# Cross part by single groups: ten chains merged by one list of turns, one or two banks per group

## The reference

```
x = x + xattn(layernorm(x), ctx)

xattn(y, Z):
  y = layernorm(y + attention(y, y, y, causal), g1, beta1)
  y = layernorm(y + attention(y, Z, Z),         g2, beta2)
  h = relu(y @ w1 + b1)                      # 128 -> 512
  y = layernorm(y + h @ w2 + b2,                g3, beta3)
```

## Time and profile before

| | |
|---|---|
| time, median of 3 runs | 762.5 us (760.36 to 763.86) |
| the profiled execution's own time | 763.72 us |
| its span, first to last instruction | 761.9 us |
| mean granted TensorE clock | 0.853 |
| busy: PE / DVE / ACT / POOL | 625.3 / 461.8 / 256.4 / 97.1 us |
| cross part, until XA is complete | about 112 us |
| DVE goes on after the trip through HBM | 123.7 us |

### The profile page before, as it was taken

How to read it: one execution, slowest core, us unless ns; L and a number is a source line. 1 busy time by engine, 2 the same in 40 slices (tenths; PEclk the granted TensorE clock), 3 DMA queues, 4 the chain that set the end, 5 groups by cost and what they waited for, 6 DMA issues and landing times.

```text
span 761.9 us, 15678 instructions
## 1 busy us (share of the span) xinstructions
PE 625.3 (82%) x6640; PEld 427.1 (56%) x6640; DVE 461.8 (61%) x1124; ACT 256.4 (34%) x555; POOL 97.1 (13%) x140
## 2 busy tenths in 40 slices
PE   2777951786899999694997699978888799999995
PEld 1434641475688858464796678776444344444442
DVE  5846694978966354748828822475556855555552
ACT  1455510742421623642632034214323122222221
POOL 2535452300000001301100001010011000000000
PEclk9888985955599999897768658976899999999998
DMA  9994021000000000000000050000032163333321
GB/s 343 291 375 160 1 83 29 0 2 2 2 3 4 3 1 3 0 3 0 2 3 2 2 178 2 2 2 1 0 80 65 57 161 94 96 97 108 88 81 28
DMA packets 18981, 46.68 MB, mean 61 GB/s; under 512 B 3456, under 2 KB 8192, under 8 KB 18656
## 3 DMA queue, kind: packets, MB, share of 16 engines
q1 hardware_dynamic: 18368, 45.43, 19.3%
q10 hardware_dynamic: 544, 0.26, 0.1%
HBM read 43.32 MB, written 2.36 MB: 60 GB/s over the span
## 4 chain that ended last, share of the span: by engine, by line
PE 66%; DVE 22%; ACT 3%; DMA 3%; POOL 2%; issue 2%; SPq 1%; DVEq 0%; POOLq 0%
PE psum L753 7%; PE psum L748 7%; PE psum L758 7%; PE psum L685 5%; PE psum L594 5%; PE psum L560 3%; PE psum L711 3%; PE psum L714 3%; PE psum L674 3%; PE psum L621 3%; PE psum L667 2%; PE psum L720 2%; PE psum L571 2%; DVE yr L1287 2%; PE psum L464 2%; DVE pcT L1287 2%
## 5 line engine op out<-in xcount | busy, mean ns | idle before, releaser
L932 ACT ACTIVATE arena<-psum 128x512 f32<-128x512 f32 x68 | 40.6, 598 | 136.0 <-PE psum L748 122.9
L1363 DVE TENSOR_TENSOR arena<-psum,arena 128x512 f32<-128x512 f32 x64 | 44.2, 691 | 59.6 <-PE psum L753 57.8
L758 PE MATMUL psum<-arena,wed_sb 128*128 128x512 f32 x128 | 66.8, 604 | 0.0
L776 ACT ACTIVATE arena<-psum 128x512 f32<-128x512 f32 x56 | 33.3, 600 | 69.7 <-PE psum L560 41.0
L1368 DVE TENSOR_TENSOR arena<-arena 128x512 f32<-128x512 f32 x64 | 44.3, 692 | 14.0 <-PE psum L758 13.8
L560 PE MATMUL psum<-arena 32*64 32x128 f32 x1024 | 41.9, 327 | 6.6 <-ACT arena L776 2.8
L952 POOL TENSOR_TENSOR ve<-ss,eps_rms 128x4 f32<-128x4 f32 x16 | 3.7, 230 | 340.5 <-ACT yr L827 252.9
L560 PEld LDWEIGHTS psum<-arena 32*64 32x64 f32 x1024 | 36.8, 165 | 12.6 <-ACT arena L776 4.1
L753 PE MATMUL psum<-yT,weu_sb 128*128 128x512 f32 x68 | 36.3, 616 | 7.9 <-DVE arena L1363 7.9
L758 PEld LDWEIGHTS psum<-arena,wed_sb 128*128 128x128 f32 x128 | 24.6, 192 | 31.3 <-issue 22.7
L1314 DVE TENSOR_TENSOR arena<-psum,small 128x1024 f32<-128x1024 f32 x24 | 28.2, 1214 | 14.2 <-PE psum L667 14.2
(11 more groups left out here) (283 smaller groups left out, 1290.2 us busy)
## 6 DMA issues: line engine op xcount, KB each, us to landing
arena<-shares SPq DMA_DIRECT2D x64, 256.0 KB, 3.9
arena<-in_ctx_t SPq DMA_DIRECT2D x16, 514.0 KB, 8.9
arena<-in_ctx_z SPq DMA_DIRECT2D x16, 512.0 KB, 10.5
XA<-in_x SPq DMA_DIRECT2D x1, 1024.0 KB, 5.1
zlast<-in_ctx_last SPq DMA_DIRECT2D x4, 256.0 KB, 17.7
x_mid<-XA SPq DMA_DIRECT2D x4, 256.0 KB, 3.0
weg_sb<-in_we_gate SPq DMA_DIRECT2D x2, 512.0 KB, 6.5
weu_sb<-in_we_up SPq DMA_DIRECT2D x2, 512.0 KB, 7.5
```

The source lines that it names most:

```text
L758: pe.matmul(x3, wed_sb[:, (p - 1) % (NPAIR + 1), :], act_a[pr], start=(p == 0), stop=False, skip_group_check=True).then_inc(x_down[pr], 1)
L776: return act.activation(out_, in_, ACT.Copy, scale=scale)
L932: act.activation(act_g[pr], banks[4 * pr + 2 * (n % 2)], ACT.Silu).then_inc(x_silu[pr], 1)
L1363: dve.tensor_tensor(act_gu[pr], banks[4 * pr + 1], act_g[pr], ALU.mult).then_inc(x_gu[pr], 1)
```

## The change

The list's steps become steps of single groups. Each pair has five chains: `BEFORE` for each of its two groups (st0 to nm1 and ev1), the attention steps c, and `AFTER` for each group (cr to fin). ev1, ev2 and fin are split off: the ACT copy to zT after the transposes (ev1, ev2), and the last update of XA (fin). One string of 76 letters takes the next step of one of the ten chains at a time: a, b, v, w are BEFORE of g0 to g3; c and x the attention steps of pair 0 and 1; d, e, y, z AFTER of g0 to g3. Semaphore counts, formerly formulas, are counted from the list by `count`. at_max, a_var and a_norm of nm0, and at_pT of sap share semaphores differently (a_vec, at_vec).

A group has two banks of its own, high (`bank + 2 + u`) and low (`bank + u`): nm0, sas, sap, nm1 use high alone, nm2 low, up both, dn high. POOL's XA + beta3 (the former L987) comes per group right behind nm2.

No instruction of the engines is added or removed but semaphore waits; shapes are the same. The core of the diff:

```
-CROSS = ["st0", "nm0", "sas", "sap", "sar", "nm1", "c0", "c1", "c2", "c3", "c4", "c5", "cr0", "c6", "c7", "c8", "c9", "cr1",
-         "nm2", "up0", "up1", "dn", "nm3"]
-XTURNS = "AABAABABBABAAAAAABABABABAABABBAABBBABBBABABBBB"
+BEFORE = ["st0", "nm0", "sas", "sap", "sar", "nm1", "ev1"]
+AFTER = ["cr", "nm2", "ev2", "up", "dn", "nm3", "fin"]
+XTURNS = ("ababwvaavabvbaawbccvbvbcwcccwvvdcwxcxccdwwexdxxxydxdeyeyxdexxdzyezyyzyeezzzz")
...
+    chains = {}
+    for pr, (g0, g1, steps, h0, h1) in enumerate(("abcde", "vwxyz")):
+        for u, name in ((0, g0), (1, g1)):
+            chains[name] = iter([(kind, u, pr) for kind in BEFORE])
+        chains[steps] = iter([("c", n, pr) for n in range(NU * GT + 2)])
+        for u, name in ((0, h0), (1, h1)):
+            chains[name] = iter([(kind, u, pr) for kind in AFTER])
+    return [next(chains[turn]) for turn in XTURNS]
...
                     if half > 0:
-                        sp.wait_ge(at_out[0], NU + n + 1)
+                        sp.wait_ge(at_out[0], count("out", 0, "c", n + 2))
...
-                    sp.wait_ge(x_done[pr], u + 1)
+                    sp.wait_ge(x_done[pr], count("done", pr, "fin", u))
...
+                g = pr * NU + u
+                low, high = banks[bank + u], banks[bank + 2 + u]
+                if kind == "nm0":
+                    pe.wait_ge(a_vec[pr], count("var", pr, kind, u))
+                    transposes(high, y, g, a_tr[pr])
...
+                elif kind == "nm2":
+                    pe.wait_ge(a_norm[pr], count("norm", pr, kind, u))
+                    pe.wait_ge(at_exp[pr], count("exp", pr, "c", NT - NU + u))
+                    transposes(low, yn, g, a_tr[pr])
+                elif kind == "up":
                     pe.wait_ge(w_in, N_WEIGHT)
...
+                    if u == 0:
+                        pe.wait_ge(at_pT[pr], NT)
...
+                        pe.matmul((high, low)[c % 2], w1_sb[:, c * P:(c + 1) * P], zT[g][:, :],
+                                  start=True, stop=True).then_inc(ff_up[pr], 1)
...
+                elif kind in ("nm1", "nm2"):
+                    k = int(kind[2])
+                    pool.wait_ge(a_norm[pr], count("norm", pr, kind, u))
+                    affine(g, (G1, G2)[k - 1], (BE1, BE2)[k - 1], st, a_scaled[pr])
+                    if k == 2:
+                        pool.wait_ge(a_scaled[pr], count("scaled", pr, kind, u) - 2)
+                        pool.tensor_tensor(r[g], y[g], bc(rowv[:, B2:B2 + 1, :], [P, GT, D]),
+                                           ALU.add).then_inc(a_scaled[pr], 1)
+                        x_g = gcols(XA, g).rearrange("p (j c) -> p j c", j=GT)
+                        pool.wait_ge(a_vec[pr], count("var", pr, "nm0", u))
+                        pool.tensor_tensor(x_g, x_g, bc(rowv[:, BE3:BE3 + 1, :], [P, GT, D]),
+                                           ALU.add).then_inc(a_scaled[pr], 1)
```

More of the change, by code:

```diff
@@ L91, in cross_schedule, with count @@
 def cross_schedule():
-    streams = [iter(CROSS), iter(CROSS)]
-    return [(next(streams["AB".index(turn)]), "AB".index(turn)) for turn in XTURNS]
-XSTEPS = cross_schedule()
+    chains = {}
[6 more added lines that the diff above has]
+    return [next(chains[turn]) for turn in XTURNS]
+XSTEPS = cross_schedule()
+ONCE = lambda *kinds: {kind: 1 for kind in kinds}
+SIGNALS = {"var": ONCE("st0", "nm0", "sar", "cr", "dn"), "rstd": ONCE("st0", "sar", "cr", "dn"),
+           "norm": ONCE("nm1", "nm2"), "scaled": {"nm1": 1, "nm2": 3}, "tr": ONCE("nm0", "nm1", "nm2", "c"),
+           "yT": ONCE("nm0", "ev1", "ev2"), "scores": ONCE("sas", "c"), "max": ONCE("sas", "sap", "c"), "exp": ONCE("sas", "c"),
+           "pT": ONCE("c"), "out": ONCE("sap", "c"), "read": ONCE("cr"), "up": {"up": FFC},
+           "h": {"up": FFC}, "ff": ONCE("dn"), "done": ONCE("fin")}
+SIGNALLING = {"scores": (0, 8), "max": (0, 8), "exp": (0, 8), "tr": (1, 9), "pT": (1, 9), "out": (2, 10)}
+def count(name, pr, kind, u):
+    total = 0
+    for k, v, p in XSTEPS:
+        if p == pr and k in SIGNALS[name] and (k != "c" or v in range(*SIGNALLING[name])):
+            total += SIGNALS[name][k]
+        if (k, v, p) == (kind, u, pr):
+            break
+    return total
 def schedule():
@@ L507, in _ @@
                     continue
-                if kind == "up0":
-                    pe.wait_ge(w_in, N_WEIGHT)
[L510 to L535, removed]
-                        for c in range(FFC):
[L537 to L548, removed]
@@ L780, in _ @@
             act.wait_ge(gb1s_made, 1)
[L781 removed]
+            for kind, u, pr in XSTEPS:
                 bank = 4 * pr
[L783 to L798, removed]
[L799 to L822 removed]
@@ new lines, in _ @@
+                if kind == "c":
+                    n = u
+                    if n < NT:
+                        act.wait_ge(at_vec[pr], count("max", pr, kind, n))
+                        if pr == 1:
+                            act.wait_ge(ca_read[0], count("read", 0, "cr", n // GT))
+                        act.activation(pc[:, n, :], banks[bank + n % 2][:, 0:KEYS], ACT.Exp, bias=nmax[pr][:, n:n + 1],
+                                       accum_out=rsum[pr][:, n:n + 1]).then_inc(at_exp[pr], 1)
+                    if 1 <= n <= NT:
+                        act.wait_ge(a_tr[pr], count("tr", pr, kind, n))
+                        copy(pcT[:, n - 1, :], banks[bank + 2][:, 0:2 * P]).then_inc(at_pT[pr], 1)
+                    continue
@@ new lines, in _ @@
+            for kind, u, pr in XSTEPS:
+                g = pr * NU + u
+                if kind in ("st0", "dn"):
+                    pool.wait_ge(a_vec[pr], count("var", pr, kind, u))
+                    rsqrt(st, g, mv[g][:, :, 1], GT, eps_ln, a_rstd[pr])
+                elif kind in ("sar", "cr"):
+                    pool.wait_ge(a_vec[pr], count("var", pr, kind, u))
+                    pool.tensor_tensor(shift[g][:, :], mv[g][:, :, 0], minus[:, :], ALU.mult)
+                    st.after(pool.tensor_tensor(ve[g][:, :], mv[g][:, :, 1], eps_ln[:, :], ALU.add))
+                    st.after(pool.tensor_tensor(rstd[g][:, :], ve[g][:, :], neg_half[:, :], ALU.pow))
+                    pool.tensor_tensor(shift[g][:, :], shift[g][:, :], rstd[g][:, :], ALU.mult).then_inc(a_rstd[pr], 1)
+                elif kind in ("nm1", "nm2"):
+                    k = int(kind[2])
[9 more added lines that the diff above has]
+                                           ALU.add).then_inc(a_scaled[pr], 1)
```

264 lines of the change are left out of this document (130 added, 134 removed).

## The result

The changed kernel took 772.01 us as median of four executions (770.28 to 773.86), the kernel before 762.51 beside it: a ratio of 1.0125, 95% interval 1.0093 to 1.0156, so slower, by about one per cent. The profiled execution took 770.28 us (span 768.5), 6.6 more than the profiled one of before. Repeated later in six executions the median was 770.52 against 763.64, +6.9.

A forecast was written before the change was run, and what follows sets the result against it. The cross part was taken as DMA-heavy first, then TensorE-bound (66.41 to 105.10 us). Last matmul +7.55, tail -1.95 and home trip +1.0 gave +6.6: 770.3 us profiled, 769.1 against the median; range 766 to 772.

The forecast's parts named there:

- Size and sign: Whole kernel: slower by 6.6 us, 770.3 for the profiled execution, 769.1 against the median; chance of slower 0.53.
- Up to c0B: nothing: Start to 48.6 us: no change, since c0B waits for saturated DMA; DVE through sar/g3 at about 47.9.
- The lock at cr/g1: DVE's four L1132 meet POOL's nm2/g0: about 5 us instead of 1.14, costing 3.7; TensorE idle 61.2 to 63.9.
- The POOL queue: Eight long operations, 82.05 to 92.8, stand before cr/g3's small ones; fin/g0 takes 5.0; the lock adds 2.2.
- The gap before nm2/g3: TensorE waits 3.6 us for ACT, then the slowed clock costs 1.5 more in dn/g2.
- rival (3): Slower still: clock stays at 0.5 through dn/g2 and up/g3, 7.5 in place of 1.5; 775.1 us, chance 0.09.
- Last feed-forward matmul: End of dn/g3 on TensorE: at 112.65 us instead of 105.1, +7.55.
- Tail on DVE and POOL: After the last matmul one group is left, not two: 4.6 us in place of 6.6, XA complete at 117.3.
- The home trip: x_mid through HBM: g2's write waits behind pair 0's loads on SP; +1.0, DVE goes on 13.0 after XA.
- The later stretch: After the cross part, 633 us before: untouched; prediction wrong if its length changes by more than 1 us.
- Rival (1): Balanced: the four L1132 of cr/g1 pass before POOL starts, later steps 5.2 earlier; 763.9 us, chance 0.27.
- Rival (2): Faster: TensorE without gaps from 58.45, DVE goes on at 119.2, POOL free earlier for cr/g3; 758.0 us, chance 0.20.

The follow-up runs named there:

- pool_g1_first: Changed kernel with one move: POOL does the long operations of nm2/g0 behind cr/g1's small ones; median 768.87 us, ratio 1.0072 to the kernel before.
- pool_g3_first: Changed kernel with one move: POOL does the long operations of nm2/g2 behind cr/g3's small ones; median 769.9 us.
- fin_g1_early: Changed kernel with nm3/g1 and fin/g1 right behind dn/g1, ahead of nm2/g3 and dn/g2; median 768.2 us.
- pool_both: Changed kernel with the POOL moves of pool_g1_first and pool_g3_first together; median 764.9 us, ratio 1.0094 to the kernel before.
- beta_early: both_fin_early with POOL's four XA + beta3 operations moved right behind sar/g2; median 758.92 us, kernel before 762.42.
- both_fin_early: Changed kernel with the moves of pool_g1_first, pool_g3_first and fin_g1_early together; median 761.29 us, kernel before 762.42.
- beta_early_again: beta_early repeated unchanged beside other kernels on one chip; median 758.05 us, kernel before 763.64, 0.9927 by medians.

## Why the prediction was right, and where it was not, point by point

- **Size and sign.** Forecast 770.3 for the profiled execution, measured 770.28; against the medians +6.6 forecast, +6.9 (and at first +9.5) measured. Of the medians, 770.52 lies inside the forecast's own 766 to 772, the first, 772.01, at its edge.
- **Up to c0B: nothing.** 48.69 against 48.56, released by the DMA as before. Right for TensorE; DVE, though, was through sar/g3 at 49.6 and not at 47.9, and in the repetition at 52.5, where cr/g1 then came 1.2 later after c0B's scores. The walk had a margin there that the runs don't show.
- **The lock at cr/g1.** Forecast 5.0, c2B's maximum at 62.8, a gap to 63.9; measured 4.91, 62.43, and 3.80 us of gap to 63.84. pool_g1_first removed it: 1.14. The four operations follow POOL's pace; shared by halves they would have taken 2 x 1.14 us. The Trainium skill (SBUF — State Buffer, section Who interferes with whom) calls the pair of ports that DVE and GpSimd share an exclusive lock; 3.2, 4.3 and 5.3 us for fin beside two, three and four long POOL operations in the versions above agree with it.
- **The POOL queue.** Eight long operations forecast from 82.05 to 92.8, measured 82.46 to 92.95; fin/g0 5.0 and 5.30; statistics of cr/g3 ready at 94.4 and 94.69. POOL idled 1.81 before cr/g3's small operations: that is the lock's part of the delay (forecast 2.2); the rest is put down to the order. pool_g3_first took away both at once, so it doesn't part them.
- **The gap before nm2/g3.** Forecast 3.6 us and 1.5 for the clock; measured 3.88 and 1.6 (5.36 against 3.74). Chosen between 0 and 7.5 by the row at 68.85, and right; up/g3 was back at full clock (3.79), so rival (3) didn't come. pool_g3_first removed both.
- **Last feed-forward matmul.** Forecast 112.65, measured 112.3 (108.48 + 3.84).
- **Tail on DVE and POOL.** Forecast 4.6, measured 4.6 (112.3 to 116.9).
- **The home trip was mis-sized.** "I add 1.0" measured +2.2: 14.2 from XA to the memsets against 12.0. The prediction's own times held more: x_mid of g2 at 117.8 with XA complete at 117.3 is 0.5 after it, where before it was 1.0 ahead, so +1.5 stood there; and the two writes of pair 1 now start together, and the first took 4.36 to land in place of 3.78. fin_g1_early showed how much hung on SP's queue: 9.3.
- **The later stretch.** "Wrong if it changes by more than 1 us": 637.4 against 638.2. This 0.8 and the matmul's 0.3 balance the trip's 1.2; the exact hit is luck to that extent. The sign itself was too sharp: in the repetition the stretch was 639.5, 1.3 more than before, and it scatters from 636.7 to 641.2 over traces that all run the same code there.
- **Rival (1)** was priced a little high and not met in either profiled execution. It let all steps behind c2B come 5.2 earlier; with the collision removed, cr/g2 came 4.5 us sooner in pool_g1_first and 3.5 in pool_both, where the granted clock was 0.55 over c2B and the start of c3B (57.69 to 61.00). **Rival (2)**, TensorE without gaps, needed what it named, POOL free before cr/g3: with it, and with cr/g1's meeting missed and the trip in order besides, beta_early went on at 117.7, near the rival's 119.2.

## What to carry to other kernels

When two engines share something exclusive, read the phase of their operations from the trace before you merge streams: one DVE step of 1.1 us became 5 beside four long POOL operations, and it did so on the path. In an in-order queue put the small operations for which others wait ahead of long ones that nobody needs yet, and take work that needs early data out of the crowd altogether. A repair at one place can shift the meeting to the next user of the same engine, so look for the next long record, not at the time alone; and before you call it a cost, compare the distance between two marks around it: fin/g1's 5.3 us beside POOL cost both_fin_early nothing against pool_both.

## What the runs showed of the hardware that was not expected

- TensorE's clock is not the same in every execution of one program: in beta_early it idled 2.06 us before c7A's transposes and was granted 0.95 from 53.95 to 62.30, in beta_early_again 2.52 us and 0.50, and the x32 output matmuls took 1.43 and 1.96. cr/g1 came 0.7 us later with it, enough to turn a near miss on the ports into a meeting of 2.1.
- After the 3.9 us gap the 32 matmuls of dn/g2 took 5.36 and 5.25 in two executions of the changed kernel and 5.67 in pool_g1_first; after 0.8 us 3.74 in pool_g3_first and pool_both.
- cr/g1's and fin's four scaled adds take 1.14 us alone, and each long POOL operation beside them holds them about 1 us longer: 3.2 beside two, 4.3 beside three, 4.9 to 5.3 beside four.
